# Wavelet stage of a two-block MetaFormer: gates computed inside the wavelet program, weights folded beside the token stage, another matmul order in a channel, scaled matrices by ScalarE

## The reference

```python
x = x + _L0_conv_ref(_ln_c(x), ...)          # 1x1, 8x8 FFT filter, depthwise 3x3, gelu gate, 1x1
t = t + _L0_ffn_ref(_ln_t(t), ...)           # per pixel 48 -> 192 -> 48, fp8 products, fp16 sums
x = x + _L1_conv_ref(_ln_c(x), ...)          # the wavelet branch, below
t = t + _L1_ffn_ref(_ln_t(t), ...)
```

```python
cx = wt_fwd(cur, wt_filt)                    # Haar: 4 bands at half size; cur = band 0
t = dwconv(t, dw_w[l])                       # depthwise 5x5 on 4*C bands
tm = einsum('coi,bcihw->bcohw', mix_w[l], tm) + mix_b[l]
gate = sigmoid(w2 @ relu(w1 @ coords + b1) + b2)      # of the pixel's coordinates alone
t = t * gate
hlow = strip_pool(t, 3); ho = hl * hlow + (1 + hh) * (t - hlow)    # 7-wide means
vlow = strip_pool(ho, 2); vo = vl * vlow + (1 + vh) * (ho - vlow)
t = t * bt + vo * gm
attn = sigmoid(sb_w[l] @ mean(t) + sb_b[l]); t = t * attn * wscale[l]
...
x_tag = inverse wavelet of both levels
base = dwconv(x, base_w, base_b) * base_scale         # 5x5
return cga_fusion(base, sigmoid(fuse_gate) * x_tag, P)
```

## Time and profile before

| | |
|---|---|
| median of 3 runs | 2807.51 us (2800.09 to 2807.88) |
| profiled execution | 2798.28 us |
| its span, first to last instruction | 2796.5 us |
| PE busy | 2339.4 us, 84% |
| DVE busy | 1596.0 us, 57% |
| ACT busy | 1013.3 us, 36% |
| POOL busy | 536.7 us, 19% |
| mean granted clock of TensorE | 0.916 |
| DMA | 454.97 MB, 163 GB/s |

### The profile page before, as it was taken

One profiled execution on the slowest core, in us unless ns is written; L12 is line 12 of the kernel. 1 busy time (PEld: TensorE's weight loads), 2 busy tenths in 40 slices (PEclk: granted clock), 3 DMA queues, 4 the chain that ended last, 5 costly groups with the idle time before them and its releaser, 6 DMA issues. The chain is left out here.

```text
span 2796.5 us, 62141 instructions
## 1 busy us (share of the span) xinstructions
PE 2339.4 (84%) x21290; PEld 1273.4 (46%) x21290; DVE 1596.0 (57%) x2838; ACT 1013.3 (36%) x1923; POOL 536.7 (19%) x833
## 2 busy tenths in 40 slices
PE   5767749999969999997399999999994999688887
PEld 2333438777743333331156666666662232233332
DVE  3334411111127777775078888888882445477776
ACT  3344411111118888884100000000000112377776
POOL 7510000000000000003055555665550000000000
PEclk9888869999989999996579999999997899799999
DMA  6987888777737777774655555555543999433332
GB/s 140 249 224 208 212 250 276 267 266 261 270 91 137 147 147 147 147 143 99 133 117 129 123 129 132 130 129 121 130 107 87 229 250 267 120 102 107 103 104 79
DMA packets 550647, 454.97 MB, mean 163 GB/s; under 512 B 335272, under 2 KB 464480, under 8 KB 547136
## 3 DMA queue, kind: packets, MB, share of 16 engines
q1 hardware_dynamic: 417490, 418.23, 57.0%
q10 hardware_dynamic: 129024, 15.75, 4.8%
q0 software_dynamic: 4032, 19.53, 2.9%
HBM read 270.23 MB, written 183.74 MB: 162 GB/s over the span
## 5 line engine op out<-in xcount | busy, mean ns | idle before, releaser
L556 PE MATMUL gate_ps<-gate_data,gate_wt 64*64 64x289 f32 x6144 | 384.3, 408 | 53.2 <-DMA gate_data<-y 39.6
L556 PEld LDWEIGHTS gate_ps<-gate_data,gate_wt 64*64 64x64 f32 x6144 | 311.9, 133 | 125.6 <-issue 60.3
L875 ACT CAST mix_h<-mix_bank 96x512 f16<-96x512 f32 x512 | 267.6, 593 | 7.0 <-PE mix_bank L826 3.2
L596 DVE TENSOR_TENSOR gate_out<-gate_gelu,gate_ps 128x578 f32<-128x578 f32 x96 | 72.6, 757 | 345.0 <-PE gate_ps L556 339.4
L1137 POOL MEMSET cg_image<- 48x7680 f32 x1 | 6.5, 6491 | 1131.7 <-POOLq L58 1131.7
L286 DVE COPY exp_out<-exp_y 128x384 f32<-128x384 f32 x192 | 102.8, 567 | 154.6 <-PE exp_y L249 153.0
L573 ACT ACTIVATE gate_gelu<-gate_ps 128x578 f32<-128x578 f32 x96 | 62.7, 653 | 351.6 <-PE gate_ps L556 351.6
L2012 PE MATMUL fus_bank<-fus_xt,fus_taps 76*32 76x512 f32 x1344 | 159.5, 626 | 27.2 <-DMA fus_shift<-gate_shift 24.3
L957 DVE TENSOR_SCALAR mix_hb<-mix_h,mix_b1q 96x1024 f16<-96x1024 f16 x256 | 122.7, 479 | 93.6 <-ACT mix_h L875 93.6
L826 PE MATMUL mix_bank<-mix_xq,mix_w1q 112*96 112x512 fp8e5 x512 | 143.5, 382 | 29.1 <-ACT mix_h L875 23.0
L965 DVE CAST mix_hq<-mix_hb 96x2048 fp8e5<-96x2048 f16 x128 | 156.5, 1223 | 19.8 <-DVE mix_hb L957 17.9
(11 more groups left out here) (220 smaller groups left out, 4316.8 us busy)
## 6 DMA issues: line engine op xcount, KB each, us to landing
y<-exp_out SPq DMA_DIRECT2D x64, 816.0 KB, 12.3
gate_data<-y SPq DMA_DIRECT2D x24, 2176.0 KB, 15.2
g<-gate_out SPq DMA_DIRECT2D x48, 578.0 KB, 3.6
mix_sc<-g SPq DMA_DIRECT2D x31, 816.0 KB
gate_wt<-wm SPq DMA_DIRECT2D x96, 256.0 KB, 4.8
wav_strips<-xp SPq DMA_DIRECT2D x96, 204.0 KB, 2.9
wav_halves<-xp SPq DMA_DIRECT2D x48, 340.0 KB, 4.4
wav_conv<-wav_lines ACTq DMA_DIRECT2D x384, 40.0 KB
```

The costliest lines, as they stand in the source:

```text
L556: mm = pe.matmul(banks(a, v)[64 * g:64 * (g + 1), r], wt[q][64 * r:64 * (r + 1), 2 * a + g, n, :], src, start=n == 0, stop=n == 3)
L875: act.copy(h16[at.pair][:, m, h, :], bank[(2 * m + h) % len(bank)][0:HID, :]).then_inc(h16_ready, 1)
```

## The change

- `coordinate_gates` is gone. `token_mix` gets a POOL block for mix0, `wavelet_weights`, which loads the tables, clears the tiles, folds the weights and writes them: the folding is POOL's now, not DVE's. The weights of `low_band` and `band_conv_0` lie in one array, `wav_front`, and one load fetches both for each half.
- `wavelet` begins with the gates: hidden layers of four column groups in one bank, then rounds of four matmuls in four row groups, each to a bank of its own, and four sigmoids. SP stores them from tiles that are used once, and then loads the first channels' gates. DVE's tables are made there too.
- PE does `up(done)` after `band_conv_0(front)` in place of `up(tail)` at the end; DVE does `add_base(done)` after `box_0`.
- ACT scales the boxes and makes the logit and base weights (`matrices_of`), POOL keeps the diagonals, the sums and `up`'s matrices. `scaled0` and `scaled1` are double.
- Half of the `conv1` loads are issued by SP.

```diff
-def coordinate_gates(nc, t, tab):
...
+def wavelet_weights(nc, pool, t, tab, k):
+    pool.dma_start(fold[:, :], t["wav_fold"]).then_inc(tables_in, 16)
...
+    pool.dma_start(front[:, :, 0:2 * STRIP], t["wav_low"].rearrange("c r p w -> c (r p) w")).then_inc(weights_out, 16)
+    pool.memset(image0[:, :, :, :], 0.0)
+    pool.memset(lines1[:, :, :, :], 0.0)
+    chain.link(pool.memset(zero[:, :, :, :, :], 0.0))
...
+    pool.wait_ge(tables_in, 16 * 22)
...
+    for l in range(2):
+        for ch in range(4):
+            for v in range(4):
+                x = pool.tensor_tensor(part[:, l, ch, :, v], ..., taps[:, l, ch].unsqueeze(3).broadcast_to([C, 5, 5, 4]), ALU.mult)
...
+    for r in range(2):
+        pool.dma_start(t["wav_front"][:, r, :, 2 * STRIP:7 * STRIP], image0[:, :, :, :].rearrange("c p t i -> c p (t i)")
+                       ).then_inc(weights_out, 16)
+    for q in range(4):
+        at = q * 4 * 20 * LINE1 + 4 - q
+        pool.dma_start(t["wav_lines"][:, at:at + 4 * 20 * LINE1 - 4], flat[:, 4:]).then_inc(weights_out, 16)
...
             @block.sync
+                for u in U:
+                    load_strips(0, u)
+                    load_conv1(0, u)
+                    load_halves(0, u)
+                for m in range(2):
+                    for g in range(4):
+                        sp.wait_ge(gate_ready, 8 * m + 4 + g + 1)
...
+                sp.wait_ge(gates_out, 16 * 20)
...
             @block.tensor
+                pe.wait_ge(coords_in, 16 * 12)
...
+                def gate_round(n, lvl, h, m, slots):
+                    pe.wait_ge(relued, h + 1)
+                    if n > 0:
+                        pe.wait_ge(gate_ready, 4 * n)
+                    for g, slot in slots:
+                        pe.matmul(gate_banks[slot][0:HID, :], cg_w2[HD * g:HD * (g + 1), lvl, HID * m:HID * (m + 1)],
+                                  hid[h][HD * g:HD * (g + 1), :], start=True, stop=True).then_inc(gated, 1)
...
                 def low_band(i, u):
-                    pe.wait_ge(in_strips[u], 96 * i + 96)
+                    pe.wait_ge(in_strips[u], 64 * i + 64)
+                    if second(i):
+                        pe.wait_ge(ct_ready, 2 * i + u - 1)
...
                     if front is not None:
                         low_band(*front)
                         band_conv_0(*front)
+                    if done is not None:
+                        up(*done)
...
-                    if tail is not None:
-                        up(*tail)
...
             @block.scalar
+                def matrices_of(i, u):
+                    n = 2 * i + u
+                    if second(i):
+                        act.wait_ge(pool_built, n - 1)
+                    for lvl, box, scaled in ((0, box0, scaled0), (1, box1, scaled1)):
+                        for m in range(2):
+                            x = act.activation(scaled[u][:, m, :], box[:, :], ACT.Copy, scale=table(coefs[lvl], n)[:, 2 + m:3 + m])
+                    x.then_inc(matrices, 1)
...
                 def step(front, tail, done):
                     if front is not None:
                         low_out(*front)
                     if tail is not None:
                         squash(*tail)
+                    if continues(front):
+                        load_conv1(front[0] + 1, front[1])
                     if front is not None:
-                        if continues(front):
-                            act.wait_ge(conv1_done, 2 * front[0] + front[1] + 1)
-                            load_conv1(front[0] + 1, front[1])
                         base_out(*front)
+                    if front is not None and (front[1] == 0 or continues(front)):
+                        matrices_of(front[0] + front[1], 1 - front[1])
...
             @block.gpsimd
                 def build_pools(i, u):
...
                     x.then_inc(pool_step, 1)
+                    pool.wait_ge(matrices, n + 1)
                     pool.wait_ge(pool_step, n + 1)
...
             @block.vector
                 def step(front, tail, done):
-                    if done is not None:
-                        add_base(*done)
                     if front is not None:
                         gate_0(*front)
                         box_0(*front)
+                    if done is not None:
+                        add_base(*done)
```

More of the change, by code:

```diff
@@ L991, in _ @@
                 staged(dve, 2 * N, SLOTS, pieces, LEAD)
+            if tab is not None:
+                @block.gpsimd
+                def _(pool):
+                    wavelet_weights(nc, pool, t, tab, k)
 LEVEL_COLS = {"mix_b": 1, "hori_low": 1, "hori_high": 1, "vert_low": 1, "vert_high": 1, "gamma": 1, "beta": 1,
@@ L1414, in store_init, with load_conv1 @@
                                  init[u][:, :, :].rearrange("y b x -> y (b x)")).then_inc(out_init[u], 16)
+                def load_conv1(i, u):
+                    c = 2 * i + u
+                    if second(i):
+                        sp.wait_ge(conv1_done, c - 1)
+                    for g in range(2):
+                        for r in range(2):
+                            sp.dma_start(*conv1_rows(c, u, g, r)).then_inc(in_conv1[u], 16)
                 for u in U:
@@ L1558, in _ @@
                 load_act_tables(nc, act, SIGMOID)
+                act.wait_ge(coords_in, 16 * 12)
+                hidden_banks = (small_bank[0], small_bank[1], full_bank[0])
+                for n in range(3):
+                    rows = slice(0, 128 if n < 2 else 2 * HD)
+                    act.wait_ge(hidden, n + 1)
+                    act.activation(hid[n][rows, :], hidden_banks[n][rows, :], ACT.Relu,
+                                   bias=cg_b1[rows, n // 2:n // 2 + 1]).then_inc(relued, 1)
@@ L1560, in load_conv1 @@
+                for m in range(2):
+                    for g in range(2):
+                        act.wait_ge(gated, 16 + 2 * m + g + 1)
+                        act.activation(gates1[m][:, 16 * g:16 * (g + 1), :],
+                                       gate_banks[2 * m + g][0:HID, :].rearrange("p (i x) -> p i x", i=16), ACT.Sigmoid,
+                                       bias=cg_b2[:, 1, m:m + 1]).then_inc(gate_ready, 1)
                 def load_conv1(i, u):
                     c = 2 * i + u
-                    for g in range(4):
+                    if second(i):
+                        act.wait_ge(conv1_done, c - 1)
+                    for g in range(2, 4):
@@ L1680, in _, with both @@
                 dve.sem_inc(finished, 2)
+                chain = Chain(dve, table_step, 0)
+                def both(make):
+                    for l in range(2):
+                        x = make(l, lambda name: levs[l][:, :, columns_of(LEVEL_COLS, name)].rearrange("p c o -> p (c o)"))
+                    chain.link(x)
+                both(lambda l, col: dve.tensor_scalar(hh[:, l], col("hori_high"), 1.0, None, ALU.add))
+                both(lambda l, col: dve.tensor_scalar(vh[:, l], col("vert_high"), 1.0, None, ALU.add))
@@ L2268, in build @@
         tab = {"levels": [table(f"levels{l}", [128, C, NLEVEL]) for l in range(2)],
[L2269 to L2272 removed]
+               "everywhere": table("everywhere", [128, C, NALL])}
+        token_mix(nc, t, "mix0", t["g"], t["woutT"], None, t["x"], t["w1T_0"], t["b1_0"], t["w2T_0"],
+                  t["b2_0"], t["x2"], t["xp"], tab)
         wavelet(nc, t, tab)
```

425 lines of the change are left out of this document (177 added, 248 removed).

## The result

The change makes the kernel slower: 2874.1 us median of four runs (2867.2 to 2893.5) against 2803.8 of the kernel before (2785.0 to 2807.9), ratio 1.029 with a 95% interval of 1.025 to 1.034. The forecast was 2757, with a range that ended at 2800. The profiled execution took 2867.2 us, its span is 2865.4, 68.9 more than before's 2796.5.

What follows compares the result with a forecast made beforehand. The prediction took the loop to be bound by a PE-VectorE circle, PE alone hardly 1 us under it. Gates -69, loop -9 and token stage +28 gave -50, so 2757 us from the 2807.5 median; range 2703 to 2800.

Steps and rivals of the forecast that it cites:

- Part 1: Gate stage removed, its work leading the wavelet block: second gating at 1349.5 in place of 1418.9, minus 69 us.
- rival D: Gate rounds: the four row groups run one after another, 8.2 us a round for 4.9, total 2774; chance 0.12.
- Part 2: Wavelet loop: PE's new order, with POOL's work slowing box_0, makes the step 14.1 us against 14.3, minus 9 us.
- the bound of 1.6: Wavelet loop: box_0 loses 1.6 us to POOL, making the step 14.6 us, plus 14 us.
- With nothing in the way the step is PE's 13.4: Wavelet loop: PE's work alone sets a 13.4 us step, minus 41 us if POOL costs nothing there.
- Rival A: Wavelet loop: VectorE's edge copies before box_0 wait for all six POOL instructions; step 16.1 us, total 2850; chance 0.08.
- Part 3: Token stage: POOL folds the weights beside it; disturbance of VectorE and of SP's queue costs plus 28 us.
- Contention: Token stage: 31 us of POOL work beside busy VectorE costs 8 us, between 0 and 31.
- The burst: Token stage: weight writes hold up SP's queue, costing 20 us, between 0 and 36.
- The lead of one or two token steps: Token stage: loads run ahead by one or two steps of 6.4 us, subtracted from about 32 us of queue hold-up.
- Rival C: Token stage pays in full, 31 + 36 us, so the whole change is minus 11, total 2796; chance 0.13.

Runs made afterwards that it cites:

- a version that clears the way: Changed kernel with weight DMAs cut and paced, ScalarE's matrices ahead of base_out, and POOL's up multiplies after weighing: 2681.0 us, ratio 0.955 to the kernel before.
- both remedies with POOL's own matrices: Changed kernel with weight DMAs cut and paced in the token stage and the scaled matrices made by POOL again: 2705.0 us, ratio 0.968 to the kernel before.
- the paced kernel: Changed kernel with POOL's clears after VectorE's casts and six big weight DMAs cut into 36, one per token step: 2818.3 us, ratio 1.006 to the kernel before.

## Why the prediction was wrong

**Part 1, the gate stage, was right.** Minus 69 forecast for the second gating; it came 52.5 us into the block in place of 125.1 after the gate stage's start, minus 72.6. First matmul at 6.4 (6.2 forecast), rounds of 4.6 us (4.9), so the four row groups do run together, and rival D is out.

**Part 2, the loop, is where it failed**, in two steps of different weight. The mechanism was there: POOL's work, released late by ScalarE's matrices, falls on box_0. I sized it at 1.1 us and it is 1.5, near the bound of 1.6; the wait for the sums became 1.3 to 1.4 us where I had 0.65, and the step at full clock 14.5 (the forecast 14.1, the bound 14.6). Had it ended there, 46 steps would have cost 11 us, inside the range. The step that failed is one that was not written down: I took every duration of PE from rows at full clock and summed them, as if the clock were a given of the stage, and put what a longer wait does to it at nothing. In this loop the clock follows PE's wait (1.00 to 0.78 with two clears put in). In the kernel before, seven of the 47 steps were already 1.2 to 2.7 us too long (0.97 in the loop), and the mean step 14.5 and not 14.3; I passed over it. A third of the loop at half clock made minus 9 into plus 85. "With nothing in the way the step is PE's 13.4" was right, and a version that clears the way gets 13.3.

**Rival A** had the sign and almost the size, a step of 16.1 and 2850, for another reason. The edge copies did wait, 0.35 and 0.26 us for 0.18 and 0.17, never for six instructions. A number near the right one from a wrong mechanism is no hit.

**Part 3, the token stage, had both mechanisms and undersized both.** Contention was put at 8 us between 0 and 31; it was 12.9, nearly all of it one cast. I had spread POOL's 31 us over many small delays of a busy loop, and had not looked at what VectorE has to do alone at the stage's start, where a single instruction stands behind 13.4 us of clears. The burst was put at 20 between 0 and 36; the stage grew by 51.6, above the upper bound. The lead of one or two token steps that I subtracted hid nothing (a token step is 6.9 us in the trace, not 6.4): the hole alone is 45.2 us, the length of the one in the earlier trace rows. And I had priced the four level-1 writes only, where two of 1,440 KB for level 0 go out ahead of them. The rest, 6 us, lies in the steps around it. Rival C (67 in all) is what happened in this stage: 64.5. The stated range was too narrow by my own bounds as well: those of the three parts add up to 2697 to 2819, and the measured 2874 lies outside even these.

The Trainium skill ("SBUF — State Buffer", Who interferes with whom) gave the argument against A: the second to issue blocks until the first has finished. The 14.67 us cast contradicts it where the other engine has several instructions in a row: it stood blocked from a DMA issue of POOL on, and through three clears that all began after it. The measurement decides; "no copy waits for more than the instruction under way" was too strong a sentence, and the 8.77 us copy of the earlier trace rows had shown so. The same skill ("DMA: Bandwidth & Descriptors", Queues, rings and completion order) has the queues served by turns, packet by packet, and I took the size of the packets for the reason of the hole. The run with small packets in a burst (3.5 KB on average in POOL's queue, for 7.7) lost as much as the one with large ones spread, so here packet size alone is not it.

In sum: minus 72 for the gates (forecast 69), plus 65 for the token stage in place of 28, plus 85 for the loop in place of minus 9. With 6.3 us less before the token stage and 2.5 less after the loop that is the difference of 69 between the two profiled executions. These two small terms are in stages that the change does not touch.

## What to carry to other kernels

A wait of PE inside a loop can cost more than its own length: where the rows show clocks under 1.00, look for the longest wait in a step and price what it does to the clock. In this loop a microsecond of delay a step cost four. When work moves from one helper engine to another, ask when its product is ready and which instructions of a third engine then run beside the ones it releases; with both moved mostly off box_0, and the writes paced, plus 2.9% became minus 4.5%. In this token stage background writes had to be both small and spread. And look whether a helper's long instructions start ahead of something short that all else waits for.

## What the runs showed of the hardware

- TensorE's granted clock went from 1.00 to 0.78 in a loop in which PE is never idle for more than 1.8 us, with nothing changed but a wait ahead of `logit` grown from 0.2 to 0.3 us to 1.4 to 1.8. With waits of 0.4 us or less in every step but the first and the last, no step was lengthened from the second on, in five traces; in a sixth (both remedies with POOL's own matrices) one was, 16.6 us for 13.9.
- The fall keeps itself, as far as these traces go. In the changed kernel steps settle at 17.05 to 17.1 us, though in them the wait is 0.66 to 0.72 us, half of what it was at full clock; with the matrices ahead of base_out one kernel ran 2757 us in one execution and 2868 in another. What it is that lets it return to full clock stays open, as does why a wait of 0.7 us does it in some stretches and not in others: length, place in the step, the matmuls around it and phase were not told apart.
- VectorE's cast of 48x192 elements, begun 0.35 us into a DMA issue of POOL, ended only after three POOL clears that followed, 14.67 us for 0.25. In the paced kernel the same cast, begun 0.09 us into that issue, took 0.25, and the next of its size 1.36, until the issue ended. Why the one passed and the other did not is open.
